# Twelve one-column comparisons in 16 bits in place of one broadcast comparison, in the edge sort of the first graph layer

## The reference

```python
# first graph layer (rows come sorted)
gathered = edge_vals[:, None] * x[cols]                       # 50000 x 256
new_x = jax.ops.segment_sum(gathered, rows, num_segments=3125)
out1 = new_x @ hamilton1                                      # then batch norm, tanh, @ hamilton2
...
# gate of the mixture that follows: 32768 edges, unsorted, plus one loop per node
src, dst = edge_index[0] + loops, edge_index[1] + loops
e = leaky_relu(a_src[src] + a_dst[dst])
ee = jnp.exp(e - segment_max(e, dst)[dst])
alpha = ee / (segment_sum(ee, dst)[dst] + 1e-16)
agg = segment_sum(h[src] * alpha[:, :, None], dst)
```

## Time and profile before

| | us |
|---|---|
| median of 3 runs | 2825.48 (2815.58 to 2832.08) |
| the profiled execution, device time | 2822.73 |
| its span, first to last instruction | 2820.9 |
| PE busy | 2125.6 (75% of the span) |
| DVE busy | 1787.4 (63%) |
| POOL busy | 1529.9 (54%) |
| ACT busy | 1123.3 (40%) |
| L1006, 416 scatters on POOL | 684.6 busy, 163.5 idle ahead of them |

### The profile page before, as it was taken

The page is one execution under the profiler, slowest core; times in us unless marked ns, Lnnn a source line. Parts: engine busy times, 40 slices in busy tenths (PEclk is TensorE's granted clock), DMA queues, the critical chain, the costliest instruction groups (busy, mean ns, idle before and its releaser), DMA issues. The chain is left out here.

```text
span 2820.9 us, 49472 instructions
## 1 busy us (share of the span) xinstructions
PE 2125.6 (75%) x10310; PEld 1616.9 (57%) x10311; DVE 1787.4 (63%) x4382; ACT 1123.3 (40%) x2764; POOL 1529.9 (54%) x1278
## 2 busy tenths in 40 slices
PE   4587777877776278999996767777777775679990
PEld 2465555655554156777784435555555554569990
DVE  5466677777668353333535848888888887654436
ACT  0354444444442042222323126666666662213332
POOL 0288888888887201777530037777777770025550
PEclk8677787787777587999997888999999998769995
DMA  7577777778777621232124457676666673532225
GB/s 250 150 111 127 120 128 132 124 126 128 130 119 103 155 66 51 46 75 61 45 77 159 149 169 207 194 203 200 201 196 201 199 197 97 190 125 70 71 67 187
DMA packets 257818, 381.37 MB, mean 135 GB/s; under 512 B 36246, under 2 KB 186181, under 8 KB 257477
## 3 DMA queue, kind: packets, MB, share of 16 engines
q0 software_dynamic: 109808, 194.70, 34.0%
q1 hardware_dynamic: 128021, 155.22, 18.3%
q10 hardware_dynamic: 19904, 30.41, 3.1%
HBM read 264.28 MB, written 115.94 MB: 135 GB/s over the span
## 5 line engine op out<-in xcount | busy, mean ns | idle before, releaser
L1006 POOL DMA_INDIRECT sum_tab<-Vs,spot x416 | 684.6, 1646 | 163.5 <-issue 100.1
L2424 POOL DMA_INDIRECT KV<-kv_tab,iS x448 | 472.6, 1055 | 183.6 <-issue 110.3
L893 PE MATMUL psV<-XN,Bs 128*128 x832 | 327.4, 506 | 167.9 <-issue 149.5
L893 PEld LDWEIGHTS psV<-XN,Bs 128*128 128x128 f32 x832 | 160.2, 233 | 306.1 <-issue 299.9
L2612 PE MATMUL psO<-msg,hot 128*128 128x264 f32 x896 | 228.5, 399 | 77.6 <-DVE agg L2532 56.3
L2600 PE MATMUL psQ<-Qs,hotT 128*128 x904 | 241.5, 414 | 56.2 <-issue 38.7
L972 ACT COPY Vs<-psV 128x512 f32<-128x512 f32 x208 | 121.6, 586 | 296.4 <-DMA sum_tab<-Vs,spot 242.8
L2612 PEld LDWEIGHTS psO<-msg,hot 128*128 128x128 f32 x896 | 165.4, 194 | 129.1 <-issue 104.8
L2600 PEld LDWEIGHTS psQ<-Qs,hotT 128*128 128x128 f32 x904 | 172.4, 203 | 108.8 <-issue 82.1
L1393 POOL DMA_INDIRECT ST<-h_tab,src x192 | 183.9, 958 | 58.5 <-issue 58.5
L2462 DVE TENSOR_TENSOR KV<-KV,psQ 128x1024 f32<-128x1024 f32 x112 | 136.7, 1221 | 77.4 <-issue 36.8
(11 more groups left out here) (592 smaller groups left out, 4380.6 us busy)
## 6 DMA issues: line engine op xcount, KB each, us to landing
kb<-key_rows SPq DMA_DIRECT2D x104, 256.0 KB
lowB<-low_tab SPq DMA_DIRECT2D x30, 512.0 KB
sum_tab<-zeros ACTq DMA_DIRECT2D x52, 256.0 KB, 3.0
parts<-sum_tab SPq DMA_DIRECT2D x20, 640.0 KB
ye_tab<-Ye SPq DMA_DIRECT2D x20, 640.0 KB, 3.5
Y<-ye_tab SPq DMA_DIRECT2D x20, 640.0 KB
lowB<-sort_tab SPq DMA_DIRECT2D x23, 384.0 KB, 6.0
keyB<-sort_tab SPq DMA_DIRECT2D x22, 384.0 KB, 5.3
```

The costliest lines, as they stand in the source:

```text
L893: ins = nc.tensor.matmul(psV[:, r % 2, x, :], Bs[:, q % 2, 2 * h + x, :], XN[:, bass.ds(t, 1), :].rearrange("p a d -> p (a d)"), start=Tru ...
L1006: pool.indirect_dma_start(out=sum_tabs[k], out_offset=bass.IndirectOffsetOnAxis(ap=spot[:, s, u:u + 1], axis=0), in_=Vs[:, j % VR, :], in_ ...
L2424: pool.indirect_dma_start(out=KV[:, s, u, :], out_offset=None, in_=kv_tab, in_offset=bass.IndirectOffsetOnAxis(ap=iS[:, s, u:u + 1], axis= ...
```

## The change

`onelo` was one VectorE instruction of 1536 elements per partition, which compares two float32 operands, both broadcast views: `iota_free` repeated twelve times, and twelve columns of `lo`, each repeated 128 times. It becomes twelve instructions of 128 elements, each of which compares `iota_h` (float16) with one column of `lo` given as a per-partition scalar. What is written, and where, is the same. This is done in `build` (23 calls) and in `tally` (24 calls). `onehi` stays as it was.

```diff
 # build(k, s, nth), L697
-v.tensor_tensor(onelo[:, s, :, :], iota_free[:, :].unsqueeze(1).broadcast_to([P, JS, P]),
-                lo[:, cols].unsqueeze(2).broadcast_to([P, JS, P]), ALU.is_equal)
+for u in range(JS):
+    v.tensor_scalar(onelo[:, s, u, :], iota_h[:, 0:P], lo[:, bass.ds(k * JS + u, 1)], None, ALU.is_equal)
 v.tensor_tensor(onehi[:, s, :, :], ...).then_inc(onesies, 1)

 # tally(n, s), L766
-v.tensor_tensor(onelo[:, s, :, :], iota_free[:, :].unsqueeze(1).broadcast_to([P, JS, P]),
-                lo[:, cols].unsqueeze(2).broadcast_to([P, JS, P]), ALU.is_equal)
+for u in range(JS):
+    v.tensor_scalar(onelo[:, s, u, :], iota_h[:, 0:P], lo[:, bass.ds(n * JS + u, 1)], None, ALU.is_equal)
 v.tensor_tensor(onehi[:, s, :, :], ...).then_inc(tallies, 1)
```

## The result

The median fell from 2824.32 to 2805.34 us (6 runs each), a ratio of 0.993, 95% interval 0.9917 to 0.9943: 19 us, faster by more than 0.5%. The forecast was 2801, its sum 24.6 us. The profiled execution took 2808.48 us, the highest of the six. All times in this text are of executions with a granted TensorE clock of 0.83 to 0.86; one execution of e11, 2941.32 us at 0.753, is left out.

What follows compares the result with a forecast made beforehand. The prediction took GpSimd's scatters to bound the phase. 27.4 us of stalls at `onelo` less 2.8 at `onehi` gave 24.6 us off, for a median of 2801 us; the 8-in-10 range was 2788 to 2817.

Steps and rivals of the forecast that it cites:

- GpSimd bounds the phase, and a scatter's length goes into the time: In the changed phase, GpSimd's 416 scatters take 684.6 us; the other engines are ahead, only about 15 us is waiting.
- Scatters wait for `onelo` to end, 27.4 us: In placing and counting, scatters stand until `onelo` ends: 19.5 us plus 7.9 us, 27.4 of 38.5 us above the median.
- the two-port rule: Skill page's rule, cited against the change: VectorE's two-port modes, entered by narrow one-source comparisons, exclude GpSimd; nothing would be gained.
- The new run lets scatters pass: In `build` and `tally`, scatters beside the twelve comparisons take the usual 1.55 us, as beside 24 similar instructions in `choose`.
- Twelve take 2.1 us, VectorE pays 19 us, hidden: In `build` and `tally`, VectorE grows slower by 0.4 us a call, 19 us over 47 calls, hidden by idle time.
- What remains is 2.8 us at `onehi`: Scatters still meet `onehi`, a 0.47 us two-operand comparison, losing 0.06 us a call, 2.8 us over 47 calls.
- The rest is not touched: Other scatter losses stay: 4.4 us for one closing scatter, two such as 2.13 us, small ones in `count_on`.
- The last scatter near 917 us: Sign expected in the changed profile: the phase's last scatter near 917 us, against a start at 941.3 before.
- a run that holds GpSimd as a whole: Rival: a scatter caught in the twelve comparisons waits for the last; 16 us slower, 2841 us; 7 in 100.
- The halved stall: Rival: each scatter meeting the new comparisons loses 0.28 us, 15 us in all; gain 9.7, 2816 us; 12 in 100.
- the next wait: Rival: faster GpSimd meets a table's last scatter not landed or an empty ring; no change, 2825 us; 6 in 100.
- VectorE as the bound: Rival: VectorE's longer `tally` in the counting stretch costs 38 us at most, less the gain, 2839 us; 2 in 100.

Runs made afterwards that it cites:

- e11: Changed kernel with twelve two-source `onelo` comparisons, each followed by a one-source `onehi` comparison of 32 elements: 2820.11 us, ratio 0.9988 to the kernel before.
- e2: Changed kernel plus an unused one-source reduction of 1536 elements behind each of the 47 `onehi`: 2817.51 us in one run.
- e1: Changed kernel with each of the twelve `onelo` comparisons again reading two float32 operands in SBUF: 2876.36 us, ratio 1.016 to the kernel before.
- e4: Kernel before with the change made in `tally` alone, `build` left as it was: 2818.95 us, ratio 0.9971 to the kernel before.
- e5: Kernel before with the change made in `build` alone, `tally` left as it was: 2807.01 us, ratio 0.9944 to the kernel before.
- e3: Changed kernel plus two unused one-source comparisons of 1536 elements in a two-port form in each `choose`, 44 in all: 2816.33 us in one run.
- e10: Changed kernel with `split`'s subtraction cut into four and the closing steps' comparison L829 cut into four: 2870.32 us, ratio 1.0158 to the kernel before.
- e7: Changed kernel with `split`'s subtraction (L735, 384 elements) cut into four of 96: 2798.06 us, ratio 0.9901 to the kernel before.

## Why the prediction was right, point by point

- *GpSimd bounds the phase, and a scatter's length goes into the time*: shown. In the changed kernel and the twelve runs the last scatter ends earlier or later than in the kernel before by what the scatters' busy time changed, to within 8 us (e2: 12); e1's 53 us more of busy time are 57 at the end. The rest is idle time ahead of scatters, 138 to 152 us against 140.3.
- *Scatters wait for `onelo` to end, 27.4 us*: shown for the place by e4 and e5. (The 23 rows of the placing stretch come to 19.2 us rather than 19.5, and one of them, 0.28 us, began in `onehi`.) The reason given was too narrow. The prediction held that two sources in SBUF are what stops a scatter, and that the trace differs from what the Trainium skill's page says. Two sources in SBUF do stop one, as L705 with one operand in PSUM doesn't. But one-source instructions stop one too: e3 showed the two-port rule at work on long ones, and in the kernel before the cast L734 had done so, 0.17 us each time. What the changed comparisons have in their favour is that they are both short and of a form that lets GpSimd in between.
- *The new run lets scatters pass*: right; the scatters that start among the twelve take 1.54 to 1.60 in the changed kernel's trace.
- *Twelve take 2.1 us, VectorE pays 19 us, hidden*: 2.0 us and 17.2 (1787.4 to 1804.6 busy), hidden.
- *What remains is 2.8 us at `onehi`*: near enough; `onehi` and what is left at `onelo` came to some 4 us in all.
- *The rest is not touched*: this is the term that was mis-sized. The sum put the change in the other losses at nothing, and the loss at `split` grew from 3.7 to 8.6 us. With `onelo` in the way, scatters started at other moments of the block; without it, twelve instead of one start in the subtraction. So 20.1 us came off the scatters instead of 24.6.
- *The last scatter near 917 us*: it started at 925.9. Besides the 4.5 us above, idle time ahead of the scatters grew by 5 us (140.3 to 145.5), most of it after 850 us. The phase so ended 15 us earlier in the one execution that has a trace, the slowest of its six; the medians differ by 19.0, inside the forecast's own range of 15 to 28.
- *The rivals*: a run that holds GpSimd as a whole did not come, yet e1 shows it as real for two-source pieces, and far dearer (53 us) than the 16 us set for it. The halved stall, the next wait, and VectorE as the bound did not come.

## What to carry to other kernels

Where GpSimd issues the transfers that bound a stretch, look at what VectorE does at the moment at which a slow transfer starts, and cut or change the long instructions there that read two operands from SBUF, or one in a fast two-port form; afterwards look for the next one that the transfers meet. Short pieces help only if GpSimd gets in between them; twelve two-source ones of 128 elements without a gap kept it out. And when a version with a few more instructions is suddenly much slower, compare phase by phase: the loss may lie in a later loop whose code only moved.

## What the runs showed of the hardware that was not expected

- Two-source instructions one after the other without a gap, some forty of them, kept one scatter waiting for 9.8 us (e1). Why four pieces of `split` (0.225 us start to start) let scatters in, and twelve pieces of `onelo` (0.20) did not, is not settled.
- Whether a loop's instructions are fetched again depends on where the loop lies: three more VectorE instructions ahead of it cost 72 us (e10 against e7), with 50 packets on the instruction queue in 550 us of the loop instead of none. The same appeared in the placing loop with the change itself (57 packets instead of 10), where it was hidden. Where the border lies, and what it is measured in, these runs don't tell.
- A two-source instruction of 0.69 us with one operand in PSUM (L705) held no scatter, in 106 that started inside it; a two-source one of 0.82 us with both in SBUF (L735) held twelve in the changed kernel, 0.55 to 0.57 us each. The two also differ in operation and type; no run moved an operand of `onelo` itself into PSUM.
